# A graph network kernel: edge windows of 20 groups of 128 edges instead of 10 of 256, and one-hots from TensorE and ACT instead of VectorE

## The reference, cut to what matters

```python
a_s = (xh * att_src).sum(-1)
a_d = (xh * att_dst).sum(-1)
alpha = jax.nn.leaky_relu(a_s[src] + a_d[dst], NEG_SLOPE)
amax = jax.ops.segment_max(alpha, dst, num_segments=n)
e = jnp.exp(alpha - amax[dst])
z = jax.ops.segment_sum(e, dst, num_segments=n)
out = jax.ops.segment_sum(xh[src] * (e / (z[dst] + 1e-16))[:, :, None], dst, num_segments=n)
```

## Time and profile before

| | us |
|---|---|
| median of 3 runs | 7659.41 (7658.97 to 7662.24) |
| the profiled execution, and its span | 7658.34, 7656.4 |
| first gather of the first edge phase | 252.1 |
| the first edge phase, first gather to last add | 252.1 to 2377.2 |
| mean granted clock of TensorE | 0.751 |

### The profile page before, as it was taken

How to read it: one execution, slowest core, us unless ns; L and a number is a source line. 1 busy time by engine, 2 the same in 40 slices (tenths; PEclk the granted TensorE clock), 3 DMA queues, 4 the chain that set the end, 5 groups by cost and what they waited for, 6 DMA issues and landing times. The chain is left out here.

```text
span 7656.4 us, 113586 instructions
## 1 busy us (share of the span) xinstructions
PE 5492.3 (72%) x23859; PEld 3669.8 (48%) x23860; DVE 5058.0 (66%) x13667; ACT 2558.7 (33%) x7905; POOL 5156.8 (67%) x5441
## 2 busy tenths in 40 slices
PE   3587777777776577777777776577878877673498
PEld 1354454444444355555544444355555544442397
DVE  4466666666667577777776667577777776668643
ACT  1322222222222333334332223244444432223465
POOL 1577777777774677777777773677777777771443
PEclk8777877877767677777777767687787777776699
DMA  4555555554543444444444444444444444444444
GB/s 121 157 145 142 143 145 141 145 139 136 140 138 102 119 120 123 121 123 123 122 116 112 112 110 122 120 123 129 129 126 129 127 119 111 112 110 142 131 71 92
DMA packets 547591, 955.11 MB, mean 125 GB/s; under 512 B 126946, under 2 KB 380876, under 8 KB 546827
## 3 DMA queue, kind: packets, MB, share of 16 engines
q0 software_dynamic: 260256, 692.79, 34.5%
q1 hardware_dynamic: 283451, 253.69, 11.0%
q10 hardware_dynamic: 3296, 2.36, 0.1%
HBM read 801.28 MB, written 155.92 MB: 125 GB/s over the span
## 5 line engine op out<-in xcount | busy, mean ns | idle before, releaser
L1213 POOL DMA_INDIRECT edges_G<-rows,edges_index x4980 | 4721.0, 948 | 1661.9 <-issue 1482.3
L1425 PE MATMUL edges_ps_o<-edges_G,edges_OH 128*128 128x264 f32 x9960 | 3561.9, 508 | 1200.2 <-DVE acc L1684 1197.0
L1425 PEld LDWEIGHTS edges_ps_o<-edges_G,edges_OH 128*128 128x128 f32 x9960 | 2319.0, 250 | 1989.8 <-DVE acc L1684 1367.0
L1263 ACT ACTIVATE edges_OHT<-edges_ps_far 128x512 bf16<-128x512 f32 x1245 | 740.9, 595 | 2299.6 <-PE edges_ps_far L1385 2299.5
L1666 DVE TENSOR_TENSOR edges_G<-edges_G,edges_ps_c 128x1024 f32<-128x1024 f32 x1245 | 1503.2, 1208 | 0.0
L1684 DVE TENSOR_TENSOR acc<-acc,edges_ps_o 128x264 f32 x2490 | 1060.1, 426 | 299.3 <-DVE acc L1684 162.2
L1565 DVE TENSOR_TENSOR edges_tu<-edges_ad,edges_G 128x80 f32<-128x80 f32 x249 | 75.1, 301 | 1255.5 <-DMA edges_G<-rows,edges_index 1255.5
L1385 PE MATMUL edges_ps_far<-edges_rels,pole_rows 5*128 5x512 bf16 x1245 | 618.8, 497 | 344.4 <-ACT edges_OHT L1263 301.8
L1658 DVE TENSOR_TENSOR edges_OH<-edges_ps_c,relT 128x512 f32<-128x512 f32 x1245 | 846.0, 680 | 0.6 <-ACT edges_ps_c L1240 0.5
L1385 PEld LDWEIGHTS edges_ps_far<-edges_rels,pole_rows 5*128 5x128 bf16 x1245 | 117.6, 94 | 976.8 <-issue 497.6
L1232 ACT ACTIVATE edges_node<-terms 128x12 bf16 x2490 | 476.1, 209 | 143.2 <-issue 89.0
(11 more groups left out here) (360 smaller groups left out, 6057.8 us busy)
## 6 DMA issues: line engine op xcount, KB each, us to landing
edges_G<-rows,edges_index POOLq DMA_INDIRECT x4980
xslot<-edges_blank SPq DMA_DIRECT2D x80, 650.0 KB
edges_masks<-lanes SPq DMA_DIRECT2D x249, 96.0 KB
rows<-node_ext SPq DMA_DIRECT2D x147, 130.0 KB, 2.3
experts_X<-xslot SPq DMA_DIRECT2D x105, 130.0 KB, 2.1
node_rows<-rows SPq DMA_DIRECT2D x98, 130.0 KB, 2.2
h<-node_Hn SPq DMA_DIRECT2D x98, 128.0 KB, 1.7
W<-in_L_ffn_W SPq DMA_DIRECT2D x16, 512.0 KB
```

The costliest lines, as they stand in the source:

```text
L1213: g.indirect_dma_start(G[n][:, s, 0:RW], None, dr["rows"], bass.IndirectOffsetOnAxis(index[n][:, s:s + 1], 0)).then_inc(gathered[n], 16)
L1263: a.activation(OHT[:, 4 * k:4 * k + 4, :].rearrange("p s e -> p (s e)"), ps_far[:, :], ACT.Relu, bias=1.0, scale=-1.0).then_inc(oht_ready, 1)
L1425: mm = pe.matmul(ps_o[BANK_OF[g]][:, 0:GW], OH[:, 2 * g + j, :], G[n][:, 2 * g + j, :], start=(j == 0), stop=(j == 1))
```

## The change

A group becomes 128 edges with a block of its own. 1563 groups of edges and 49 blocks make 81 windows of 20 groups, so an edge phase has 1620 gathers instead of 1660. The constant WG goes; the block numbers of a window take two words.

In an edge phase:

- PE's 20 matmuls of a window stay, but each is a group by itself and has its own add: 20 adds a window instead of 10. The three banks are used in rotation.
- `load_node` makes 20 copies a window instead of 10, and reads two words instead of one; so does DVE for its adds.
- DVE's five `onehots` a window go. In their place PE makes, for each of five chunks, four matmuls of 5x128 by 5x128 (`distances_on_edges`) into the same `ps_far`, and ACT turns them into `OH`, still one buffer of 20 slots.
- the rows of powers (`rels`) are kept for four windows instead of two.

In the walk, three arrays of edges become one array of triples, so that 13 indirect DMAs replace 21; the destinations are read from the input instead of from a copy; the group numbers are turned with 13 small matmuls; and the links leave in 2 DMAs instead of 28.

The core of the diff (the walk's part is cut):

```diff
-GE = 2 * P
+GE = P
-WG = 10
-WS = 2 * WG
-NW = -(-(TG + NB - 1) // WG)
+WS = 20
+HG = WS // 2
+NW = -(-(TG + NB - 1) // WS)
...
+        def bank(w, g):
+            return ps_o[(WS * w + g) % BANKS][:, 0:GW]
...
-            word = eng.value_load(words[0:1, bass.ds(w, 1)], min_val=0, max_val=64 * 2 ** (WG - 1) - 1)
-            b = eng.snap(word & 63)
-            for g in range(WG):
+            for half in range(2):
+                word = eng.value_load(words[0:1, bass.ds(2 * w + half, 1)], min_val=0, max_val=64 * 2 ** (HG - 1) - 1)
+                b = eng.snap(word & 63)
+                for g in range(HG):
...
+            def onehots(i, n):
+                w = RING * i + n
+                for k in range(CHUNKS):
+                    a.wait_ge(near_ready, FAR * w + k + 1)
+
+                    wait_past(a, summed, WS * (w - 1) + 4 * k + 4)
+                    a.activation(OH[:, 4 * k:4 * k + 4, :].rearrange("p s e -> p (s e)"), ps_far[:, :], ACT.Relu,
+                                 bias=1.0, scale=-1.0).then_inc(oh_ready, 1)
...
                 if exists(i, n, 1):
                     fades(*later(i, n, 1))
+                    onehots(*later(i, n, 1))
...
+            def distances_on_edges(i, n, k):
+                w = RING * i + n
+                if k == 0:
+                    pe.wait_ge(oht_ready, FAR * min(w + 3, NW))
+
+                wait_past(pe, oh_ready, FAR * w + k)
+                r, at = rows_of(n)
+                for s in range(4):
+                    mm = pe.matmul(ps_far[:, s * P:(s + 1) * P], rels[r, at, (4 * k + s) * P:(4 * k + s + 1) * P], pole[r, :],
+                                   start=True, stop=True)
+                mm.then_inc(near_ready, 1)
...
-                    wait_past(pe, added, WG * w + g + 1 - since_bank(g))
-                    for j in range(2):
-                        mm = pe.matmul(ps_o[BANK_OF[g]][:, 0:GW], OH[:, 2 * g + j, :], G[n][:, 2 * g + j, :],
-                                       start=(j == 0), stop=(j == 1))
-                    mm.then_inc(summed, 1)
+                    wait_past(pe, added, WS * w + g + 1 - BANKS)
+                    pe.matmul(bank(w, g), OH[:, g, :], G[n][:, g, :], start=True, stop=True).then_inc(summed, 1)
...
-            def onehots(i, n, k):
-                w = RING * i + n
-
-                wait_past(v, summed, WG * (w - 1) + 2 * k + 2)
-                rel = relT[:, bass.ds(w * WG + 2 * k, 2), :].rearrange("p g j -> p (g j)")
-                v.tensor_tensor(OH[:, 4 * k:4 * k + 4, :], ps_iota.unsqueeze(1).broadcast_to([P, 4, P]),
-                                rel.unsqueeze(2).broadcast_to([P, 4, P]), ALU.is_equal).then_inc(oh_ready, 1)
```

More of the change, by code:

```diff
@@ L127, in prepare_walk @@
     pad_rows = TG + 1
+    whole = E // GE
+    rest = E - whole * GE
+    assert 1 < rest < GE and whole + 1 == TG
     with Phase(nc, "walk") as ph:
[L129 to L131 removed]
+        pad = ph.sb("pad", [1, 3, P], I32)
         dstI = ph.sb("dstI", [P, TC, GE], I32)
@@ L195, in prepare_walk @@
         block = ph.block()
[L196 to L210, removed]
+        QUARTERS = 4
+        rowT = NG // QUARTERS
@@ L212, in _ @@
+        assert NG % QUARTERS == 0 and rowT <= 512
+        triples = dr["triples"]
+        sources = ((dst, 0), (dst, 1), (src, 0))
         @block.sync
         def _(sp):
[L214 to L218, removed]
@@ L1790, in step @@
                     add(i, n, 0, b)
+                    add(i, n, 1, next(blocks))
                     next(extra, None)
-                    add(i, n, 1, next(blocks))
+                    for g in (2, 3):
+                        add(i, n, g, next(blocks))
                 if one:
@@ L1806, in step @@
                 if here:
-                    add(i, n, 4, next(blocks))
+                    for g in (8, 9):
+                        add(i, n, g, next(blocks))
                 next(extra, None)
@@ L1811, in step @@
                 if here:
-                    add(i, n, 5, next(blocks))
+                    for g in (10, 11):
+                        add(i, n, g, next(blocks))
                 if two:
@@ L1823, in step @@
                 if here:
-                    add(i, n, 6, next(blocks))
+                    for g in (12, 13):
+                        add(i, n, g, next(blocks))
                 if two:
@@ L1827, in step @@
                 if here:
-                    add(i, n, 7, next(blocks))
+                    for g in (14, 15):
+                        add(i, n, g, next(blocks))
                 if two:
@@ L1836, in step @@
                     place_drops(*next2)
-                if one:
-                    onehots(*next1, 2)
                 if here:
-                    add(i, n, 8, next(blocks))
+                    for g in (16, 17):
+                        add(i, n, g, next(blocks))
                 if one:
@@ L1843, in step @@
                 if here:
-                    add(i, n, 9, next(blocks))
+                    for g in (18, 19):
+                        add(i, n, g, next(blocks))
                 for _ in extra:
```

357 lines of the change are left out of this document (170 added, 187 removed).

## The result

The changed kernel takes 9396.89 us (median of 4 runs, 9372.73 to 9402.31) against 7659.19 (7658.87 to 7662.24): 1.2263 times as long, 95% interval 1.2246 to 1.228. The forecast was 9260, the range 8700 to 9780. The profiled execution is the shortest of the four, 9372.73 us.

The account below looks back on a forecast made before the run. POOL's gathers were taken to pace the kernel before, and a loop DVE, PE, ACT, DVE the changed one. 7658.3 + 1639 (edge phases) - 39 (walk) = 9258, say 9260 us; range 8700 to 9780.

Parts of the forecast that it names:

- POOL paces before, and not after: Edge phases: gathers on POOL set 25.07 us a window before; afterwards POOL runs ahead, then waits for the sums.
- The loop DVE, PE, ACT, DVE with the copies in it: Edge window: ACT's twenty copies follow the fifth one-hot, so this loop sets 30.0 us instead of 25.07; chance 0.72.
- F to T = 21.4: Edge window, start of `fade_sums` to end of the 17th add: 19.4 us without waits plus 2.0 waiting for ACT's fade.
- waits of adds for PE's sums: Sign of being wrong: new waits inside DVE's run of adds, for `edges_ps_o`, would make PE the bound.
- T to F' = 8.6: End of 17th add to next `fade_sums`: last sum, distances, fifth one-hot, twenty copies, exponentials and DVE's start, 8.6 us.
- the intervals of 30.0: Edge windows without attention block, one `fade_sums` to the next: 21.4 + 8.6 = 30.0 us, 29 a phase.
- The intervals with the block, 31.1, 34.4, 36.2: Windows with attention block in layers 0, 1, 2, 49 a phase: ACT's block work before the copies lengthens them.
- Tails of 62 us: Last three windows of each edge phase, without the copies: 62 us instead of 40.5.
- The walk, -39: Walk before the edge phases: fewer link and indirect DMAs, destinations not copied; -39 us, between -20 and -45.
- POOL pacing: Rival: gathers still set the edge interval if the loop is shorter than 25.07; 7530 us, chance 0.08.
- DVE pacing: Rival: DVE, not ACT, sets the edge interval, 26.5 us, 27 with the block in layers 1 and 2; 7915, chance 0.09.
- PE at its low clock all along: Rival: PE never returns to full clock in the edge windows, +2.2 us on 234 intervals; 9775 us, chance 0.09.

Follow-up runs that it names:

- the copies between the one-hots: Against the changed kernel: ACT's twenty node copies spread in fours ahead of the five one-hots instead of behind them; 8772.24 us, ratio 1.1438.
- the one-hots on DVE: Changed kernel's walk and groups of 128, but one-hots on DVE as before and no distances on edges; 8514.62 us, ratio 1.1104.
- the best order of the move: Against the changed kernel: node copies between the one-hots, and ACT's part of the attention block ahead of the one-hots; 8438.19 us, ratio 1.1024.

## Why the prediction was right

The profiled execution is 115 us over the 9258 of the sum: the edge phases are 118 longer than it said, the walk and the rest 4 shorter. The median is 24 us above the profiled execution.

- *POOL paces before, and not after.* Right: the wait for the gathers is gone, and a gather still takes 946 ns. Where the idle time of POOL would be seen was wrong in one point: it was to be "idle some 5 us a window for `edges_ps_o`", but the profile puts 245.0 us there and 3019.8 under "issue".
- *The loop DVE, PE, ACT, DVE with the copies in it.* Right without the block and in layer 1, and shown by two runs: the copies moved out of it, and halved in it. In layer 2 the copies carry 1.0 to 1.5 us of the interval, and with the block in layer 0 nothing.
- *F to T = 21.4.* Measured 21.7, 21.9 and 22.0 without the block, 19.6 in layer 0 with it, 21.7 in layers 1 and 2. Two errors nearly offset each other in it: the wait for ACT's fade is 1.5 to 1.7 without the block, not 2.0, and there are waits of adds for PE's sums, 395.2 us over the program (62.8 before), which the prediction had named as a sign of being wrong. Most of them are the 0.37 that the wait for the add before would take too; what goes beyond 0.4 in each adds up to some 107 us, 0.4 a window, so they don't make PE the bound.
- *T to F' = 8.6.* Mis-sized: 9.5, 9.3 and 9.5 on average. The fifth one-hot starts at T + 1.7 to 1.9, not 1.25. The four distances, for which no row had a price, were about right: the one-hot starts 0.6 behind their start. It is the last sum that was priced too low, 0.6 at full clock: from its first matmul to the distances it takes 0.9 to 1.0, at a granted clock of 0.62 in 2000 to 2500 us. And between the two runs of ten copies lie 0.78 us, not 0.5. So the intervals of 30.0 are 31.2 to 31.5: 29 x (1.2 + 1.2 + 1.5) = 113 us of the 118.
- *The intervals with the block, 31.1, 34.4, 36.2.* Measured 30.7, 34.8, 36.7; over all 49 of each phase 4976 us where the prediction had 4984. But the reason given, that DVE's own wait for the differences "ends earlier than ACT's chain", fails in layer 0 and holds narrowly in layer 2. PE in layer 0 after the fifth one-hot (1511.77 on ACT), then DVE and ACT:

```profile
1513.55 0.80 PE L1457 MATMUL edges_ps_r<-edges_v,edges_high 128*128 128x130 f32 x2 [1.81 <-ACT edges_ex L1290]
...
1515.44 3.32 PE L1439 MATMUL edges_ps_m<-WT,edges_xm 128*128 128x512 f32 x4
1518.61 0.27 PE L1395 MATMUL edges_ps_s<-ident,edges_greatest 128*128 128x128 f32 x1
```

```profile
1518.92 0.24 DVE L1641 TENSOR_TENSOR edges_diff<-edges_alpha,edges_ps_s 128x80 f32<-128x80 f32 x1 [6.02 <-PE edges_ps_s L1395]
```

```profile
1519.19 0.24 ACT L1208 ACTIVATE edges_ps_c<-edges_diff 128x80 f32<-128x80 f32 x1 [0.37 <-DVE edges_diff L1641]
```

  ACT is done with its copies and waits 0.37 us for the differences, which wait for PE's part of the block. On average the differences start at T + 9.0 and the exponentials at T + 9.5 in layer 0, at 11.9 and 13.3 in layer 2. That is why the copies between the one-hots gave nothing in layer 0 and 1.0 in layer 2. The 31.1 of layer 0 came out by luck: F to T was 1.8 shorter than said and T to F' 1.4 longer, for a reason (PE) that the prediction had set aside.
- *Tails of 62 us.* From the `fade_sums` of the 79th window of the first phase (2698.8) to the end of its last add (2758.7): 59.9.
- *The walk, -39.* Measured -40.1. Its largest term, 23.8 for the link DMAs, was somewhat smaller: from their issue to the first load of the node phase it is now 7.6 us instead of 27.8, 20.2 less; the other walk edits then gave 19.9 where 15 were counted. SP in the changed kernel:

```profile
74.01 0.89 SPq L226 DMA_DIRECT2D links<-walk_links  x2
81.57 0.37 SPq L542 DMA_DIRECT2D node_X<-in_x  x1
```

- *The rivals.* POOL pacing would have needed 25.6 an interval; the best of these kernels has 26.6. DVE pacing, 26.5 computed, is about what is left when the copies are out of the loop and no block runs: 26.6 to 27.3. PE at its low clock all along didn't come true, though the last sum behind T is closer to the low clock's price than to the full one's (0.9 to 1.0, between 0.58 and 1.06). The granted clock is lower than before, 0.686 over the span where it was 0.751:

```profile
500.00:1500.00 1000.00, 819.08 (x3277) 435.29 (x3277) 605.90 (x1524) 394.96 (x1279) 613.46 (x649) 0.76 0.42 118
2000.00:2500.00 500.00, 389.31 (x1414) 200.37 (x1413) 290.08 (x728) 172.42 (x558) 300.55 (x318) 0.62 0.40 111
...
6100.00:7300.00 1200.00, 963.48 (x3563) 555.20 (x3563) 662.16 (x1729) 546.21 (x1475) 617.03 (x653) 0.65 0.32 87
```

These stretches of the changed kernel (us, busy of PE, PEld, DVE, ACT, POOL, granted clock, DMA) have 0.76 with the block in layer 0, where F to T is shortest (19.6) and DVE waits least for ACT's fade, 0.65 with it in layer 2, and 0.62 without it; the earlier trace rows alternated between 0.50 and 1.00. That the clock is what makes the 19.6 is argued from this and was not tested.

## What to carry to other kernels

Before work is moved to an idle engine, write down that engine's queue in order: work that waits late for another engine puts everything queued behind it on the path, here twenty copies and the exponentials that had been free, while ACT was busy for a third of the span. If it must wait late, put the rest of the step in front of it, which gave back about 959 of the 1726 us here (9396.89 less 8438.19, against 9396.89 less 7671.0). And look first whether the engine that is relieved paces at all: in the kernel before it didn't, and even where it did, with the one-hots on DVE at 8514.62, the best order of the move gained 76 us.

## What was not expected of the hardware

The same kernel before took 7659 and 7671 us on two occasions, and 9111, 9033, 9037 and 9103 on four others, on three chips (the last two on one of them), each within 0.4% of its median. The kernel before itself was not traced on these; nearest to it are the two runs with only the shorter walk. The busy times hardly tell them apart: in the first run with the short walk end (9098.43 us) a gather takes 954 ns instead of 948, and the granted clock is 0.738 instead of 0.751. From the first gather to the first `fade_sums` that kernel takes 140.9 us instead of 78.2, and an interval is about 30 us instead of 25. The time is in stalls that hit several engines together. The profile names no wait for many of them, and for others transfers of a node phase, which aren't part of an edge phase: DVE's adds stand 1300.0 us for `xnT<-node_hT`. In that run ACT's copies, which come every 0.25 us, at one place come every 4, and DVE's adds stand still with them:

```profile
1054.69 0.21 ACT L1229 ACTIVATE edges_node<-terms 128x12 bf16 x1 [1.36 <-issue]
1057.60 0.21 ACT L1229 ACTIVATE edges_node<-terms 128x12 bf16 x1 [2.69 <-issue]
1061.82 0.21 ACT L1229 ACTIVATE edges_node<-terms 128x12 bf16 x1 [4.01 <-issue]
1066.03 0.21 ACT L1229 ACTIVATE edges_node<-terms 128x12 bf16 x1 [4.00 <-issue]
```

```profile
1058.86 0.43 DVE L1681 TENSOR_TENSOR acc<-acc,edges_ps_o 128x264 f32 x1 [5.50 <-DMA xnT<-node_hT]
...
1067.01 0.43 DVE L1681 TENSOR_TENSOR acc<-acc,edges_ps_o 128x264 f32 x1 [5.39 <-DMA xnT<-node_hT]
```

Some 45 us earlier PE stands between sums without a wait:

```profile
1009.33 0.86 PE L1422 MATMUL edges_ps_o<-edges_G,edges_OH 128*128 128x264 f32 x2
1011.95 0.38 PE L1422 MATMUL edges_ps_o<-edges_G,edges_OH 128*128 128x264 f32 x1 [1.76 <-issue]
1012.70 0.79 PE L1422 MATMUL edges_ps_o<-edges_G,edges_OH 128*128 128x264 f32 x1 [0.36 <-issue]
```

No run here tells what stalls them, and how the changed kernel does on such a chip wasn't measured. A ratio of two kernels holds for the chip on which both ran.
